# A decoder layer whose split products read their moving tiles backwards, with weight places displaced

## The chip, the cores and the metric

The kernel runs on one core of a Trainium2 chip. The metric is the device time of one execution in microseconds (us). Below, PE is TensorE, PEld its weight load, DVE is VectorE, ACT ScalarE, POOL GpSimd and SP SyncE.

## The reference

The kernel computes one decoder layer for 2 sequences of 512 tokens with 1024 features: a selective-scan (Mamba) block, a cross-attention and a feed-forward part, each added to its input and followed by a layer norm.

```python
def reference(x, ctx, ...):                       # x [2,512,1024], ctx [2,1024,1024]
    # 1: in_proj -> conv over 4 tokens, silu -> x_proj, norms, dt -> scan over 16 states -> gate -> out_proj
    proj = x @ in_proj_w; x1, z = split(proj)
    xc = silu(conv(x1)); dt, B, C = rmsnorms(xc @ x_proj_w.T); dt = softplus(dt @ dt_w + bias)
    h_t = exp(dt_t * A) * h_{t-1} + dt_t * B_t * xc_t;  y_t = h_t . C_t
    x = layernorm(x + ((y + D * xc) * silu(z)) @ out_proj_w.T)
    # 2: 16 query heads of 96 over 4 key/value heads, keys from [ctx, x] (1536 rows)
    x = layernorm(x + softmax(q k^T / sqrt(96)) v @ Wo.T)
    # 3: weights scaled by blocks of 128 x 128, 1024 -> 3584 -> 1024
    x = layernorm(x + (silu(x @ (w1*s1).T) * (x @ (w3*s3).T)) @ (w2*s2).T)
```

All is float32. Products are to come out with more precision than one float32r product gives.

## The kernel before, in words

**Split products.** A float32 operand is split into a part that ACT rounds to float32r (`hi`) and the remainder that DVE or POOL subtracts (`lo`). A product is then three float32r matmuls into one PSUM bank, issued by the helper `three_passes` (line 106): `w_hi` times `x_hi` (L108), `w_hi` times `x_lo` (L109), `w_lo` times `x_hi` (L110). The first operand is the weight tile of 128 columns, loaded before each matmul (PEld); the second is the moving tile, mostly of 512 columns, which streams past it.

**Who uses the helper.** The input projection (`mamba_in`, with the small x_proj product of 96 weight columns among it), the output projection (`steps`), keys, values and queries, attention's probabilities times values, the output projection of attention, and the feed-forward part. Attention's scores (L1961 to L1963) and its row maxima (L1939) are float32r matmuls too, but are issued directly. The scan (L972 to L1019) uses plain float32 matmuls.

**Where the tiles lie.** Each phase places its SBUF tiles one behind another with an `Arena` (line 79), which rounds each tile's size up to 32 bytes. Tiles of the split products are multiples of 512 bytes, so weights and moving tiles lie at the same place modulo 512 bytes in nearly every phase. The exception is the x_proj product, whose weight tiles are 384 bytes long, one behind another (`xpw_hi`, `xpw_lo`).

**Order.** There is no scheduler. Every engine has a function of its own for each phase, with its loops and semaphore waits written out. In the feed-forward part, `NW = 8` slots of `w_hi` and `w_lo` go round: ACT rounds into `w_hi` (L2377, in the second half L2401), DVE subtracts into `w_lo` (L2566, L2614), PE waits for `w_lo_done` and runs 12 matmuls (4 tiles of K, three passes each). The first half makes 7 products per pair of blocks in place of 8, with DVE and POOL making sums of operands and results; the second half reads its operands back from device memory. In `mamba_in` two slots of `w_hi` and `w_lo` go round (L334 on ACT, L407 on DVE), 48 matmuls of PE to each.

Of the kernel before, what the change touches and what calls it, by code (L numbers as in the profile page):

```python
# [22 lines left out]
F32R = mybir.dt.float32r  # L23
# [4 lines left out]
P = 128  # L28
B, L, H = 2, 512, 1024
TOK = B * L  # L30
HT = H // P
# [71 lines left out]
    return ap.bitcast(F32)  # L103


def three_passes(nc, out, w_hi, w_lo, x_hi, x_lo, start, stop):

    nc.tensor.matmul(out, w_hi, x_hi, start=start, stop=False)  # L108
    nc.tensor.matmul(out, w_hi, x_lo, start=False, stop=False)  # L109
    return nc.tensor.matmul(out, w_lo, x_hi, start=False, stop=stop)  # L110
# [92 lines left out]
def mamba_in(nc, res, d, ps_all, scan):  # L203
# [6 lines left out]
    sb = Arena(nc, "in")  # L210
# [8 lines left out]
    x_hi = sb("x_hi", [P, HT, TOK], F32R)  # L219
    x_lo = Arena(nc, "in")("x_lo", [P, HT, TOK], F32R)  # L220
    dtw = Arena(nc, "in_dtw", sb.at)("dtw", [R + 1, IT, P])
    w = [sb(f"w{s}", [P, HT, P]) for s in range(2)]
    w_hi = [sb(f"w_hi{s}", [P, HT, P], F32R) for s in range(2)]
    w_lo = [sb(f"w_lo{s}", [P, HT, P], F32R) for s in range(2)]
    xz = [sb(f"xz{s}", [P, B, L + KC - 1]) for s in range(2)]
    acc = [sb(f"acc{s}", [P, B, L]) for s in range(2)]
    pre = [sb(f"pre{s}", [P, B, L]) for s in range(2)]
# [261 lines left out]
    def tensor(pe):  # L489
        def main(m, s, between=None, at=0):  # L490
            pe.wait_ge(w_lo_done, m + 1)
            pe.wait_ge(left, m)
            for k in range(HT):
                pe.wait_ge(x_lo_done, k + 1)
                if between is not None and k == at:
                    between()
                for b in range(B):
                    c = slice(b * L, (b + 1) * L)
                    last = three_passes(nc, ps[s][:, b], w_hi[s][:, k], w_lo[s][:, k], x_hi[:, k, c], x_lo[:, k, c],
                                        k == 0, k == HT - 1)  # L500
            last.then_inc(main_done, 1)

        def xproj(s, ready, stop=False):
            pe.wait_ge(xc_lo_done, ready)
            pe.wait_ge(xpw_done, ready)
            for b in range(B):
                last = three_passes(nc, ps_xp[:, b], xpw_hi[s][:], xpw_lo[s][:], xc_hi[s][:, b], xc_lo[s][:, b],
                                    False, stop)
            last.then_inc(xproj_done, 1)
# [522 lines left out]
def mamba(nc, res, d, steps):  # L1032
# [3 lines left out]
    scan = mamba_scan(nc, res, d, ps_all, steps)  # L1036
    early = Phase(nc)
    first = mamba_in(nc, early, d, ps_all, scan)

    with nc.Block() as block:  # L1040
# [187 lines left out]
def project_norm_qkv(nc, res, d, ps, heads, steps):  # L1228
# [322 lines left out]
    def tensor(pe):  # L1551
        def step(n):
            s, k = n % 2, n
            pe.wait_ge(steps.lo_done, 2 * n + 2)
            for m in range(HT):
                c = slice(m * P, (m + 1) * P)
                last = three_passes(nc, ps[:, m], steps.w_hi[s][:, c], steps.w_lo[s][:, c], steps.a_hi[s][:], steps.a_lo[s][:], k == 0, k == KT - 1)
                if k == KT - 1:
                    last.then_inc(tile_done, 1)
                    if m == FIRST:  # L1560
                        pe.wait_ge(const_set, 2)
                        pe.wait_ge(v_done, HT + 2)
                        mean(0)
            if k < KT - 1:
                last.then_inc(steps.used, 1)
# [434 lines left out]
def heads_and_feed_forward(nc, res, d, steps, carried, attn, out, ahead):  # L2000
# [7 lines left out]
    with nc.Block() as block:  # L2008
        @block.sync
        def _(sp):  # L2010
            nonlocal forward
            first.sync(sp)
            heads.sync(sp, lambda: (early.release(), carried.release()))

            forward = attention_out_feed_forward(nc, res, d, ps, heads, attn, out, ahead)
            forward.sync(sp)
# [26 lines left out]
def attention_out_feed_forward(nc, res, d, ps, heads, attn, out, ahead):  # L2043
# [11 lines left out]
    NJ = FT // 2  # L2055
    NM = 7
    NW, NX = 8, 4
    sb = Arena(nc, "ff")

    def sem(n):  # L2060
# [4 lines left out]
    x_hi, x_lo, x_at = [None] * NM, [None] * NM, [0] * NM  # L2065
# [36 lines left out]
    w_hi, w_lo = [], []  # L2102
    for s in range(NW):
        if s == NW - 1:
            wo_at = Arena(nc, "ff_wo", sb.at)
        w_hi.append(sb(f"w_hi{s}", [P, HK, P], F32R))
        w_lo.append(sb(f"w_lo{s}", [P, HK, P], F32R))
    p0, u3 = sb("p0", [P, L]), sb("u3", [P, L])
    u2, u4 = ([sb(f"{n}{s}", [P, L]) for s in range(2)] for n in ("u2", "u4"))
    wo[0] = wo_at("wo0", [P, KH, P])  # L2110
# [971 lines left out]
```

## Time and profile before

| | us |
|---|---|
| two runs | 3046.60 and 3050.18, median 3048.39 |
| profiled execution: first to last instruction | 3047.5 |
| PE busy | 2833.3 (93%), 11958 matmuls |
| DVE busy | 2393.1 (79%) |
| POOL busy | 1712.8 (56%) |
| ACT busy | 1574.6 (52%) |

The profile gives the busy time of each engine, the granted clock of TensorE, groups of instructions by line, the waits, and a timeline. The duration of a matmul in it includes its way through the array, and matmuls overlap: how long one occupies the engine is read from the distance between the starts of two.

The phases on PE, from the timeline: input projection up to 220 us, the small dt products up to 318, the scan up to 1114, output projection, keys, values and queries up to 1418, attention up to 2041, its output projection up to 2178, the feed-forward part to the end, its second half from 2748.

### The profile page before, as it was taken

The numbers are of one execution on the slowest core, as the hardware profiler recorded it, in microseconds if no ns is written. First come the engines' busy times: TensorE is split into PE (matmuls) and PEld (weight loads), VectorE is DVE, ScalarE is ACT, GpSimd is POOL, SyncE is SP. The second block draws the span as 40 slices with busy tenths as digits, with TensorE's granted clock in tenths as the row PEclk, the third lists the DMA queues.
The fourth block names the chain that finished last, engine by engine and source line by source line (L and its number), as shares of the span: only waits on it lengthen the run. The fifth ranks groups of instructions, "written<-read, shape, count | busy, mean of one in ns | idle before, by whom it ended". The sixth has DMA issues, their size and how long they took to land. (4 is left out here: it accounts for less than half of the span.)

```text
span 3047.5 us, 35696 instructions
## 1 busy us (share of the span) xinstructions
PE 2833.3 (93%) x11958; PEld 2028.4 (67%) x11958; DVE 2393.1 (79%) x2168; ACT 1574.6 (52%) x2685; POOL 1712.8 (56%) x1035
## 2 busy tenths in 40 slices
PE   8997588888788889999999999999989999999997
PEld 7882244444222348888888888887768888887886
DVE  6558999999999977444777777765988888885677
ACT  4448555555665545213888888873433333334443
POOL 0003999999999953403888888861044444430034
PEclk9995799999999999999999999999989999999999
DMA  4228886666875645232111111215245555567654
GB/s 152 83 83 261 274 200 159 179 171 152 250 219 148 199 150 216 104 119 72 37 37 37 37 37 37 71 54 200 97 156 180 180 179 180 180 218 238 194 176 139
DMA packets 217641, 445.84 MB, mean 146 GB/s; under 512 B 33661, under 2 KB 47741, under 8 KB 215613
## 3 DMA queue, kind: packets, MB, share of 16 engines
q1 hardware_dynamic: 179742, 390.73, 41.1%
q10 hardware_dynamic: 37728, 52.96, 5.3%
q8 instruction: 91, 1.49, 0.2%
q14 instruction: 80, 0.66, 0.1%
HBM read 313.45 MB, written 130.15 MB: 146 GB/s over the span
## 5 line engine op out<-in xcount | busy, mean ns | idle before, releaser
L1927 POOL TENSOR_TENSOR at_p_lo<-at_p,at_p_hi 128x512 fp32r<-128x512 f32 x384 | 514.6, 1348 | 244.3 <-ACT at_p_hi L1820 236.5
L716 POOL TENSOR_TENSOR scan_dbx<-scan_u,scan_b_bc 128x1024 f32<-128x1024 f32 x256 | 596.1, 2359 | 0.0
L885 ACT ACTIVATE mamba_ps<-scan_dt,scan_a_neg 128x512 f32<-128x512 f32 (+1 forms) x512 | 332.0, 680 | 315.1 <-DVE scan_g L903 291.3
L914 DVE TENSOR_TENSOR_SCAN mamba_ps<-mamba_ps,scan_dbx 128x1024 f32<-128x1024 f32 x195 | 440.0, 2283 | 3.1 <-ACT mamba_ps L887 1.7
L1847 DVE TENSOR_REDUCE at_neg_max<-heads_ps 128x1 fp32r<-128x1536 f32 x128 | 224.9, 1757 | 134.4 <-PE heads_ps L1939 132.4
L108 PE MATMUL heads_ps<-ff_x_hi,ff_w_hi 128*128 128x512 f32 x784 | 310.0, 395 | 17.2 <-DVE ff_u L2572 6.4
L2812 POOL TENSOR_TENSOR ff_raw<-ff_raw,ff_scale 128x512 f32<-128x512 f32 x112 | 115.9, 1066 | 361.2 <-DMA ff_raw<-in_w 252.8
L109 PE MATMUL heads_ps<-ff_x_lo,ff_w_hi 128*128 128x512 f32 x784 | 308.1, 393 | 0.0
L110 PE MATMUL heads_ps<-ff_x_hi,ff_w_lo 128*128 128x512 f32 x784 | 308.1, 393 | 0.0
L1816 ACT ACTIVATE at_p<-heads_ps 128x512 f32<-128x512 f32 x384 | 228.2, 594 | 110.0 <-PE heads_ps L1963 95.8
L1820 ACT ACTIVATE at_p_hi<-at_p 128x512 fp32r<-128x512 f32 x384 | 242.8, 632 | 12.2
L989 PE MATMUL mamba_ps<-scan_x,scan_wz 128*128 128x512 f32 x448 | 212.5, 618 | 23.8 <-ACT scan_zb L805 16.7
L903 DVE TENSOR_TENSOR scan_g<-mamba_ps,scan_c_bc 128x1024 f32<-128x1024 f32 x195 | 234.2, 1201 | 0.0
L1019 PE MATMUL mamba_ps<-scan_g,scan_sel 128*32 128x512 f32 x1024 | 138.9, 613 | 81.3 <-DVE scan_g L903 67.5
L989 PEld LDWEIGHTS mamba_ps<-scan_x,scan_wz 128*128 128x128 f32 x448 | 82.7, 194 | 155.7 <-issue 129.0
L108 PEld LDWEIGHTS heads_ps<-ff_x_hi,ff_w_hi 128*128 128x128 f32 x784 | 149.1, 190 | 51.5 <-DVE ff_u L2572 7.4
L109 PEld LDWEIGHTS heads_ps<-ff_x_lo,ff_w_hi 128*128 128x128 f32 x784 | 149.2, 190 | 31.5 <-issue 0.5
L110 PEld LDWEIGHTS heads_ps<-ff_x_hi,ff_w_lo 128*128 128x128 f32 x784 | 149.0, 190 | 31.3
L2377 ACT ACTIVATE ff_w_hi<-heads_ps 128x512 fp32r<-128x512 f32 x112 | 66.9, 598 | 197.2 <-DVE heads_ps L2561 183.7
L108 PE MATMUL heads_ps<-ff_hs_hi,ff_w_hi 128*128 128x512 f32 x392 | 154.7, 395 | 7.3 <-DVE ff_act_h L2601 3.7
L929 POOL TENSOR_TENSOR scan_g<-scan_g,scan_c_bc 128x1024 f32<-128x1024 f32 x61 | 144.2, 2365 | 24.5 <-DVE scan_g L914 24.4
L110 PE MATMUL heads_ps<-ff_hs_hi,ff_w_lo 128*128 128x512 f32 x392 | 153.8, 392 | 0.0
(306 smaller groups left out, 6906.8 us busy)
## 6 DMA issues: line engine op xcount, KB each, us to landing
scan_dt<-dt SPq DMA_DIRECT2D x120, 256.0 KB, 4.8
scan_u<-u SPq DMA_DIRECT2D x120, 256.0 KB, 7.6
ff_raw<-in_w SPq DMA_DIRECT2D x56, 512.0 KB, 4.6
ff_down_ar<-ac SPq DMA_DIRECT2D x98, 256.0 KB, 2.8
ff_down_hr<-hc SPq DMA_DIRECT2D x98, 256.0 KB, 2.7
ff_act_w<-in_w SPq DMA_DIRECT2D x14, 1024.0 KB, 7.6
hc<-ff_act_t SPq DMA_DIRECT2D x56, 256.0 KB, 6.2
ac<-ff_act_v SPq DMA_DIRECT2D x56, 256.0 KB, 5.9
```

What stands on the lines that cost most here:

```text
L108: nc.tensor.matmul(out, w_hi, x_hi, start=start, stop=False)
L109: nc.tensor.matmul(out, w_hi, x_lo, start=False, stop=False)
L110: return nc.tensor.matmul(out, w_lo, x_hi, start=False, stop=stop)
L716: nc.gpsimd.tensor_tensor(dbx[n % SL][:].rearrange("p (h l) -> p h l", h=2), u[it % 2][:, c:c + 2], b_bc[b][:, k // 2].unsqueeze(1).to_bro ...
L885: nc.scalar.activation(at[:, h * L + h:(h + 1) * L], dt[it % 2][:, c, h:L], ACT.Exp, scale=a_neg[:, it % IT, e:e + 1]).then_inc(a_ready, 1)
L903: nc.vector.tensor_tensor(g[n % SG][:].rearrange("p (h l) -> p h l", h=2), ps_a[n % SA].rearrange("p (h l) -> p h l", h=2), c_bc[n // (NP ...
L914: nc.vector.tensor_tensor_scan(out[:], ps_a[n % SA], dbx[n % SL][:], 0.0, ALU.mult, ALU.add).then_inc(scanned, 1)
L989: last = nc.tensor.matmul(ps_x, wz[q % ZC][:, k], x[:, k, b * L:(b + 1) * L], start=k == 0, stop=k == HT - 1)
L1816: nc.scalar.activation(p[t % NSL][:], ps_s[t % 2], ACT.Exp, scale=SCALE).then_inc(exp_done, 1)
L1820: nc.scalar.activation(p_hi[t % NSL][:], p[t % NSL][:], ACT.Copy).then_inc(p_hi_done, 1)
L1847: nc.vector.tensor_reduce(neg_max[:, i, HD:HD + 1], ps_mx.rearrange("p n l -> p (n l)"), AX_X, ALU.max, negate=True).then_inc(max_done, 1)
L1927: nc.gpsimd.tensor_tensor(p_lo[n % NSL][:], p[n % NSL][:], f32(p_hi[n % NSL][:]), ALU.subtract).then_inc(p_lo_done, 1)
```

## The change

It has two parts. `three_passes` views its output and both moving tiles from the last column to the first (`[:, ::-1]`), so that the moving tile is read, and the PSUM bank written, backwards; each result lands where it did. And weight places are displaced: in `mamba_in` the four slots get 64 bytes more room and begin 16, 48, 4 and 8 bytes into it (`w_hi0`, `w_lo0`, `w_hi1`, `w_lo1`); in the feed-forward part each of the sixteen places is followed by 32 bytes, so that they lie 0, 32, 64, ... 480 bytes past a multiple of 512. `align()` brings what follows back to a multiple of 512. No instruction is added, removed or moved on any engine, and no wait changes.

```diff
+def back(ap):
+    return ap[:, ::-1]
+
 def three_passes(nc, out, w_hi, w_lo, x_hi, x_lo, start, stop):
 
+    out, x_hi, x_lo = back(out), back(x_hi), back(x_lo)
     nc.tensor.matmul(out, w_hi, x_hi, start=start, stop=False)
     nc.tensor.matmul(out, w_hi, x_lo, start=False, stop=False)
     return nc.tensor.matmul(out, w_lo, x_hi, start=False, stop=stop)
...
-    w_hi = [sb(f"w_hi{s}", [P, HT, P], F32R) for s in range(2)]
-    w_lo = [sb(f"w_lo{s}", [P, HT, P], F32R) for s in range(2)]
+    w_hi, w_lo = [], []
+    for s in range(2):
+        for part, name, by in ((w_hi, "w_hi", (16, 4)[s]), (w_lo, "w_lo", (48, 8)[s])):
+            wide = sb(f"{name}{s}", [P, HT * P + 16], F32R)
+            part.append(wide[:, by // 4:by // 4 + HT * P].rearrange("p (k m) -> p k m", m=P))
...
+    STEP = 32
...
     for s in range(NW):
         if s == NW - 1:
-            wo_at = Arena(nc, "ff_wo", sb.at)
+            wo_at = Arena(nc, "ff_wo", sb.at).align()
         w_hi.append(sb(f"w_hi{s}", [P, HK, P], F32R))
+        sb.at += STEP
         w_lo.append(sb(f"w_lo{s}", [P, HK, P], F32R))
+        sb.at += STEP
+    sb.align()
```

## Rows read from the trace of the kernel before

**Rows 1.** Page: busy time, clock by fortieths, the chain that ended last by line.
```profile
PE 2833.3 (93%) x11958; PEld 2028.4 (67%) x11958; DVE 2393.1 (79%) x2168; ACT 1574.6 (52%) x2685; POOL 1712.8 (56%) x1035
...
PEclk9995799999999999999999999999989999999999
...
PE heads_ps L108 9%; PE heads_ps L110 9%; PE heads_ps L109 9%; DVE ff_w_lo L2614 1%; DVE ff_hs_lo L2617 1%; PE heads_ps L2998 0%; DVE ff_x_lo L2539 0%; DVE ff_y L2543 0%; DVE ff_norm_rstd L1187 0%; DMA ff_wo_wo<-in_w_o 0%; DVE ff_wo_wo_lo L2522 0%; DVE ff_y L1193 0%; DVE ff_w_lo L2566 0%; POOL ff_raw L2812 0%; ACT ff_x_hi L2356 0%
```

**Rows 2.** Busy time by stretch, columns as in its head.
```profile
core 0: us, PE busy (x) PEld busy (x) DVE busy (x) ACT busy (x) POOL busy (x), PEclk, DMA share, GB/s
10.00:220.00 210.00, 210.00 (x922) 170.42 (x921) 125.68 (x121) 95.86 (x90) 10.12 (x16) 1.00 0.27 94
...
1418.00:2041.00 623.00, 621.61 (x2802) 511.75 (x2800) 458.36 (x303) 518.23 (x874) 514.64 (x384) 1.00 0.14 41
2041.00:2228.00 187.00, 172.03 (x711) 136.06 (x712) 145.94 (x197) 73.54 (x106) 9.91 (x8) 0.97 0.42 145
2228.00:2985.00 757.00, 747.21 (x3268) 616.34 (x3268) 594.42 (x792) 265.45 (x450) 285.02 (x200) 0.99 0.57 192
```

**Rows 3.** The busiest stretch of DVE, same columns.
```profile
2400.00:2640.00 240.00, 240.00 (x1061) 198.79 (x1060) 210.31 (x281) 74.93 (x125) 112.78 (x82) 1.00 0.53 183
```

**Rows 4.** PE groups by line: count, busy us, mean ns, idle before.
```profile
L108 PE MATMUL heads_ps<-ff_x_hi,ff_w_hi 128*128 128x512 f32 x784 | 310.0, 395 | 17.2 <-DVE ff_u L2572 6.4 <-DVE ff_x_lo L2539 5.8 <-ACT ff_act_h L2396 5.0
...
L108 PE MATMUL heads_ps<-ff_hs_hi,ff_w_hi 128*128 128x512 f32 x392 | 154.7, 395 | 7.3 <-DVE ff_act_h L2601 3.7 <-DVE ff_hs_lo L2617 3.7
```

**Rows 5.** Line L108 alone in the stretches before 318 and behind 1114.
```profile
10.00:220.00 210.00, 119.89 (x307) 1.00 0.27 94
220.00:318.00 98.00, 5.86 (x14) 0.60 0.75 250
...
1114.00:1206.00 92.00, 51.57 (x128) 0.96 0.76 274
1206.00:1418.00 212.00, 116.89 (x304) 0.98 0.28 95
1418.00:2041.00 623.00, 149.55 (x384) 1.00 0.14 41
2041.00:2228.00 187.00, 94.39 (x231) 0.97 0.42 145
2228.00:2985.00 757.00, 426.31 (x1089) 0.99 0.57 192
2985.00:3047.50 62.50, 19.94 (x48) 0.90 0.37 124
```

**Rows 6.** Timeline of PE, feed-forward: start us, duration, first and last of 178 matmuls.
```profile
2599.79 0.39 PE L109 MATMUL heads_ps<-ff_x_lo,ff_w_hi 128*128 128x512 f32 x1
...
2639.91 0.39 PE L109 MATMUL heads_ps<-ff_x_lo,ff_w_hi 128*128 128x512 f32 x1
```

**Rows 7.** Timeline, one matmul and the weight load beside it.
```profile
2700.20 0.39 PE L108 MATMUL heads_ps<-ff_x_hi,ff_w_hi 128*128 128x512 f32 x1
2700.20 0.19 PEld L109 LDWEIGHTS heads_ps<-ff_x_lo,ff_w_hi 128*128 128x128 f32 x1
```

**Rows 8.** Timeline of PE, output projection, where the clock rises.
```profile
1118.16 0.63 PE L110 MATMUL heads_ps<-step_a_hi,step_w_lo 128*128 128x512 f32 x1
...
1119.87 0.63 PE L108 MATMUL heads_ps<-step_a_hi,step_w_hi 128*128 128x512 f32 x1
...
1120.61 0.40 PE L110 MATMUL heads_ps<-step_a_hi,step_w_lo 128*128 128x512 f32 x1
...
1121.32 0.39 PE L110 MATMUL heads_ps<-step_a_hi,step_w_lo 128*128 128x512 f32 x1
1121.54 0.39 PE L108 MATMUL heads_ps<-step_a_hi,step_w_hi 128*128 128x512 f32 x1
...
1122.70 0.39 PE L110 MATMUL heads_ps<-step_a_hi,step_w_lo 128*128 128x512 f32 x1
```

**Rows 9.** Timeline of PE, x_proj: first of six matmuls, and what follows them.
```profile
33.22 0.39 PE L108 MATMUL mamba_ps<-in_xc_hi,in_xpw_hi 128*96 128x512 f32 x1
...
34.60 0.39 PE L108 MATMUL mamba_ps<-in_x_hi,in_w_hi 128*128 128x512 f32 x1
```

**Rows 10.** Writers in the input projection, 10 to 220 us: count, busy us, mean ns, idle before.
```profile
L334 ACT ACTIVATE in_w_hi<-in_w 128x1024 fp32r<-128x1024 f32 x17 | 17.9, 1052 | 0.1
...
L358 ACT ACTIVATE in_xz<-mamba_ps 128x1024 f32<-128x1024 f32 x16 | 16.5, 1028 | 21.1 <-PE mamba_ps L110 21.1
```

## The prediction

> **What bounds the kernel.** I began with the page: PE is busy 93% of the span, DVE 79%, and the chain that ended last names the three lines of the helper, L108 to L110, as its largest parts; the clock is near full nearly everywhere [rows 1]. Then the stretches. Outside the scan, PE is busy 210.0 of 210 us in the input projection, 621.6 of 623 in attention and 747.2 of 757 in the feed-forward part [rows 2]. Where DVE is busiest it has 210.3 of 240 us, PE all of them [rows 3]. So outside the scan time is the number of matmuls times the distance between two starts. The idle time before L108 shows how little PE waits: 17.2 and 7.3 us over the feed-forward part's two halves [rows 4].
>
> The helper's matmuls: L108 runs 307 + 14 + 128 + 304 + 384 + 231 + 1089 + 48 = 2505 times [rows 5], with L109 and L110 7,515 in all. None is in the scan.
>
> The distance is what the change can touch. Between the first and the last of 178 matmuls lie 177 distances: 2639.91 − 2599.79 = 40.12 us, 226.7 ns each [rows 6]. At full clock (2.4 GHz) 512 columns, one a cycle, need 213.3 ns. At the lower clock (1.2 GHz) four distances take 1119.87 − 1118.16 = 1.71 us, 427 ns each, and 512 columns need 426.7: nothing is added there [rows 8]. So at full clock each matmul pays 13.4 ns above its columns, at half clock none. What goes on beside it is the next weight load, which begins with the matmul and lasts 190 ns whatever happens [rows 7]: moving reads and weight reads fall in the same time.
>
> Two rows say that this surcharge depends on how the two streams lie to each other. Behind the rise of the clock the same operands have distances of 0.22 and 0.24 us in turn, (1122.70 − 1120.61) / 9 = 232 ns on average, before they settle at 226.7 [rows 8]. And the x_proj product, whose weight tiles don't lie at the moving tile's place modulo 512 bytes, needs (34.60 − 33.22) / 6 = 230 ns, with fewer weight columns (96) to load [rows 9]. I read this as weight reads taking turns from moving reads at the same part of SBUF, and the aligned placement before as one that settles into a fairly good rhythm.
>
> **The change, part by part.** *Reading backwards.* Counts, order and waits stay. The compiled program reads weights from the last column down. Before, the two streams run against each other; now both run down, the moving one about twice as fast. They meet fewer times during a load, but may stay together longer when they do. No row of before has this. Its value is bounded by rows: below by the columns alone, 213.3 ns (13.4 saved; a gain is not excluded, since half clock shows it), above by the worst distances seen between unsettled streams, 0.24 us, of which the averages are 230 and 232 [rows 8, 9]. I take 220, the middle between 226.7 and 213.3: half of the surcharge goes. It also matches the best single distance of before, 0.22 us between 1121.32 and 1121.54 [rows 8], which shows that a better rhythm exists.
>
> Full clock holds for about 7,400 of the 7,515: the granted clock of 0.96 to 0.99 in the stretches behind 1114 [rows 5] means some 50 us at half clock, about 120 matmuls. Saved: 7,400 × 6.7 ns = 49.6 us.
>
> The direct float32r matmuls of attention keep 226.7, but for those beside which a helper's weights load.
>
> *Displacing the feed-forward places.* It changes where 1,176 × 3 helper matmuls' weights (784 + 392) [rows 4] lie to their moving tiles, in sixteen ways. By itself it could undo the rhythm, as in x_proj: that price is in the bounds above. Writers stay at multiples of 32 bytes, as x_proj's do; I add nothing.
>
> *Displacing the input projection's places by 4 to 48 bytes.* ACT and DVE now write and read there off a 32-byte multiple. The nearest row is L358, which writes 12 bytes off and takes 1028 ns against 1052 for L334 [rows 10]: no price. Even 5% on both would lie under PE, with ACT busy 96 and DVE 126 of 210 us [rows 2].
>
> *What is late next.* With 3% less PE time, DVE's 210 of 240 us becomes 210 of 233 [rows 3]; DVE doesn't bind on average, but single waits such as those before L108 [rows 4] grow. I give back 2 us.
>
> Sum: 49.6 − 2 = 48 us less. The profiled span is 3047.5, 0.9 under the median of the runs, 3048.4; from the median, 3000.
>
> **What the Trainium skill says.** By its page "TensorE: Matmul & The Clock Gate" (Step-by-step), TensorE has two independent read ports, and loading weights doesn't take read bandwidth from the running matmul. By that rule direction and place change nothing; this is the third case below. The trace disagrees with its number: it gives 215.7 ns between matmuls of 512 columns, the rows 226.7. The page "Advanced Engine Details and Errata" (PSUM Cachelines) says that an access pattern of PSUM that isn't contiguous slows matmuls significantly; neighbours remain neighbours here, but no row shows a descending write, and the last case below is what it would do.
>
> **The rivals.**
> 1. *The surcharge goes almost wholly*: 213.3 to 217.5 ns. Both streams go the same way, and once one is past the other they don't meet again. For it: half clock shows no surcharge. Against: x_proj shows that merely moving places doesn't do it. At 215.5: 7,400 × 11.2 = 83 us, less 5 given back to DVE: 2970.
> 2. *Slower: the rhythm is lost.* With the moving stream in step with the weight stream, they contend for a whole stretch of a load, and with displaced places the matmul never settles, as behind the clock's rise and in x_proj. At 232 ns: 7,400 × 5.3 = 39 us more, 3087; it decides from 226.7 up, the worst (236) gives 3117. For it: two of three placements in the rows are worse than the aligned one. Against: nothing says that direction breaks the rhythm.
> 3. *No change*: the surcharge is a fixed cost of a float32r weight load (32 cycles for 128 columns), direction and place don't matter. 225 to 229 ns: 3036 to 3065. Against it: 0.22 to 0.24 us for the same operands [rows 8].
> 4. *A descending stream runs at half rate*: 427 ns, as at half clock [rows 8], 7,400 × 0.2 us more: some 4530. For it only that no row excludes it.
>
> **How the numbers follow.** Chances: the forecast (217.5 to 225 ns, 2982 to 3036) 46%, nearly all gone 21%, no change 17%, slower by a lost rhythm 13%, half rate 3%. The predicted time is the likeliest case's. The range 2962 to 3072 leaves out the lower end of rival 1 (4%), most of rival 2 (10%) and rival 4. A measurement here tells 2%, 61 us, from no change. Faster by over 61 us needs 218.4 ns or less: rival 1 and the edge of the forecast, 29%. Slower by over 61 us needs 235 or rival 4: 6%. Within: 65%.
>
> **What would show it.** Right: in the feed-forward part 178 matmuls span about 38.9 us in place of 40.12; all float32r weight loads keep 190 ns; L1961 and L1939 keep 226.7 and the scan its time; PE stays busy all through attention and the feed-forward part. Distances that differ by slot of the ring would show that the displacement matters, equal ones that direction does. Wrong: distances of 230 or more; or distances as forecast with DVE waits before L108 that eat the gain.

## The result

| | us, median (lowest to highest) | ratio to the kernel before, 95% interval |
|---|---|---|
| kernel before | 3048.39 (3046.6 to 3050.18) | |
| changed kernel | 3101.42 (3100.01 to 3102.83) | 1.0171 (1.0142 to 1.0201) |

The changed kernel is 53 us slower, where 48 us less were forecast. Its profiled execution spans 3098.7 us against 3047.5, 51.2 us more.

The page of the changed kernel, in the form of [rows 1]:

```profile
PE 2892.5 (93%) x11958; PEld 2034.8 (66%) x11958; DVE 2384.7 (77%) x2168; ACT 1579.3 (51%) x2685; POOL 1710.6 (55%) x1035
...
PEclk9995799999989999999999999999989999999999
...
PE heads_ps L114 10%; PE heads_ps L115 9%; PE heads_ps L116 9%; DVE ff_w_lo L2627 1%; DVE ff_hs_lo L2630 1%; DVE ff_x_lo L2552 0%; DVE ff_y L2556 0%; PE heads_ps L3011 0%; POOL ff_raw L2825 0%; DVE ff_y L1202 0%; PE heads_ps L1156 0%; DVE ff_norm_rstd L1196 0%; DVE ff_sum_y L2814 0%; DVE ff_w_lo L2579 0%; POOL ff_end_total_sq L2899 0%
...
L114 PE MATMUL heads_ps<-ff_x_hi,ff_w_hi 128*128 128x512 f32 x784 | 316.8, 404 | 15.8 <-DVE ff_u L2585 6.5
...
L114 PE MATMUL heads_ps<-ff_hs_hi,ff_w_hi 128*128 128x512 f32 x392 | 158.4, 404 | 6.3 <-DVE ff_act_h L2614 3.5
```

PE is busy 59 us longer with the same 11,958 matmuls, of which the span shows 51, since PE idles 8 us less; DVE, ACT and POOL have what they had to within 9 us, and the clock row is the same but for one slice. The chain still consists of the helper's three lines, now L114 to L116. The waits before the first of them have become shorter, from 17.2 and 7.3 us to 15.8 and 6.3 [rows 4]. So no wait and no engine beside PE took the time: each matmul takes longer.

The stretch of [rows 3] again:

```profile
2400.00:2640.00 240.00, 240.00 (x1029) 193.11 (x1028) 200.00 (x269) 73.91 (x123) 110.05 (x80) 1.00 0.52 178
```

The timeline of PE in the feed-forward part, as [rows 6] (start us, duration us), first and last of 173 matmuls:

```profile
2649.69 0.40 PE L116 MATMUL heads_ps<-ff_x_hi,ff_w_lo 128*128 128x512 f32 x1
...
2689.86 0.40 PE L114 MATMUL heads_ps<-ff_x_hi,ff_w_hi 128*128 128x512 f32 x1
```

The weight load there, from the timeline of PE's loads, as [rows 7]:

```profile
2649.93 0.19 PEld L115 LDWEIGHTS heads_ps<-ff_x_lo,ff_w_hi 128*128 128x128 f32 x1
```

PE is busy all of 240 us in both kernels, at a granted clock of 1.00, but gets through 1029 matmuls where it did 1061. Between the first and the last of the 173 matmuls lie 172 distances: 40.17 us, 233.5 ns each, against 226.7 [rows 6]. The weight load keeps its 0.19 us [rows 7]. At full clock (2.4 GHz) 226.7 ns are 544 cycles, 32 above the 512 columns; 233.3 ns are 560, or 48 above. So what a matmul takes above its columns, the surcharge, grew by a half; the forecast had it halved.

Where the clock rises, in the output projection, the changed kernel looks like this (PE, start us, duration us), to be read beside [rows 8]:

```profile
1124.36 0.63 PE L115 MATMUL heads_ps<-step_a_lo,step_w_hi 128*128 128x512 f32 x1
...
1126.49 0.45 PE L114 MATMUL heads_ps<-step_a_hi,step_w_hi 128*128 128x512 f32 x1
1126.78 0.40 PE L115 MATMUL heads_ps<-step_a_lo,step_w_hi 128*128 128x512 f32 x1
...
1131.91 0.40 PE L116 MATMUL heads_ps<-step_a_hi,step_w_lo 128*128 128x512 f32 x1
```

At half clock five distances take 1126.49 − 1124.36 = 2.13 us, 426 ns each: reading backwards costs nothing there, just as the surcharge was nil before. At full clock the 22 distances from 1126.78 on take 5.13 us, 233.2 ns each, from the first one. There is no unsettled stretch that settles later; this is the steady state.

By stage, from the timelines (us; distances are medians of the helper's matmuls in the stage, in whole ns, as the trace has the starts). The input projection is taken up to the first of the small dt products, at 231.5 us in the kernel before, not to the 220 us named ahead:

| stage | before | after | more | distance before | after |
|---|---|---|---|---|---|
| input projection | 231.5 | 238.4 | 6.9 | 227 | 233 |
| dt and scan | 883.1 | 884.1 | 1.0 | | |
| output projection | 91.9 | 93.5 | 1.6 | 227 | 233 |
| keys, values, queries | 211.7 | 216.7 | 5.0 | 227 | 233 |
| attention | 623.5 | 637.3 | 13.8 | 227 | 231 to 240 by line |
| its output projection | 135.6 | 138.1 | 2.5 | 227 | 233 |
| feed-forward, first half | 570.2 | 584.9 | 14.7 | 227 | 231 to 236 by slot and line |
| feed-forward, second half | 300.0 | 305.7 | 5.7 | 227 | 231 to 236 by slot and line |

The scan has plain float32 matmuls and doesn't use the helper: nothing happened there. Every other stage pays.

Attention pays more than its share, since there both directions occur. The timeline of PE before, the first direct matmuls of a group:

```profile
1600.04 0.39 PE L1961 MATMUL heads_ps<-at_q_hi,at_k_hi 128*128 128x512 f32 x1
1600.27 0.39 PE L1962 MATMUL heads_ps<-at_q_lo,at_k_hi 128*128 128x512 f32 x1
1600.50 0.39 PE L1963 MATMUL heads_ps<-at_q_hi,at_k_lo 128*128 128x512 f32 x1
```

The same piece of the changed kernel, with the helper's three behind it:

```profile
1602.08 0.40 PE L1970 MATMUL heads_ps<-at_q_hi,at_k_hi 128*128 128x512 f32 x1
1602.32 0.39 PE L1971 MATMUL heads_ps<-at_q_lo,at_k_hi 128*128 128x512 f32 x1
1602.55 0.39 PE L1972 MATMUL heads_ps<-at_q_hi,at_k_lo 128*128 128x512 f32 x1
1602.78 0.40 PE L114 MATMUL heads_ps<-at_p_hi,at_v_hi 128*128 128x512 f32 x1
1603.01 0.40 PE L115 MATMUL heads_ps<-at_p_lo,at_v_hi 128*128 128x512 f32 x1
1603.25 0.40 PE L116 MATMUL heads_ps<-at_p_hi,at_v_lo 128*128 128x512 f32 x1
```

L1970 to L1972 are the old L1961 to L1963, and are themselves not reversed. Still the distance from L1970 to L1971 went from 0.23 to 0.24 us (median 227 to 238 ns over 384 pairs). The distances behind the helper's three lines sum to 8.3 us more, near the 1,152 × 6.7 ns = 7.7 us that a flat rise would give; those behind the direct matmuls, which the change doesn't touch, sum to another 5.6 us, 2.0 of it in the row maxima.

### The profile page after: what moved, and what is told of

It is laid out like the page before. It is cut to its first block and busy times, and to the rows that moved or that the text cites. A ratio compares the mean times of both kernels' runs of the same rounds, so it can differ in the third digit from the quotient of the medians.

```text
span 3098.7 us, 35696 instructions
## 1 busy us (share of the span) xinstructions
PE 2892.5 (93%) x11958; PEld 2034.8 (66%) x11958; DVE 2384.7 (77%) x2168; ACT 1579.3 (51%) x2685; POOL 1710.6 (55%) x1035
## 5 line engine op out<-in xcount | busy, mean ns | idle before, releaser
L114 PE MATMUL heads_ps<-ff_x_hi,ff_w_hi 128*128 128x512 f32 x784 | 316.8, 404 | 15.8 <-DVE ff_u L2585 6.5
L115 PE MATMUL heads_ps<-ff_x_lo,ff_w_hi 128*128 128x512 f32 x784 | 314.9, 402 | 0.0
L116 PE MATMUL heads_ps<-ff_x_hi,ff_w_lo 128*128 128x512 f32 x784 | 314.3, 401 | 0.0
L114 PEld LDWEIGHTS heads_ps<-ff_x_hi,ff_w_hi 128*128 128x128 f32 x784 | 149.6, 191 | 55.1 <-DVE ff_u L2585 7.4
L115 PEld LDWEIGHTS heads_ps<-ff_x_lo,ff_w_hi 128*128 128x128 f32 x784 | 149.7, 191 | 36.4 <-issue 0.5
L116 PEld LDWEIGHTS heads_ps<-ff_x_hi,ff_w_lo 128*128 128x128 f32 x784 | 149.4, 191 | 36.5
L114 PE MATMUL heads_ps<-ff_hs_hi,ff_w_hi 128*128 128x512 f32 x392 | 158.4, 404 | 6.3 <-DVE ff_act_h L2614 3.5
L115 PE MATMUL heads_ps<-ff_hs_lo,ff_w_hi 128*128 128x512 f32 x392 | 157.6, 402 | 0.0
```

## The experiments

Two theories stood after the result. **Direction:** reading the moving tile from its last column down is what costs, whatever the places. **Places:** the displaced weights cost, and direction does little or even helps. Behind them stood a third question, whether it is the read or the backward write into PSUM, and whether the weight load has a part in it at all.

**Reading backwards alone**, all places as before:

```diff
+def back(ap):
+    return ap[:, ::-1]
...
 def three_passes(nc, out, w_hi, w_lo, x_hi, x_lo, start, stop):
 
+    out, x_hi, x_lo = back(out), back(x_hi), back(x_lo)
```

> Kernel before with the moving tiles and PSUM output of the helper reversed, all places as before. Theory A (direction: both streams going down settle into a dearer rhythm): 233.3 ns between helper matmuls in every phase, 3095 to 3101 us. Theory B (the displaced places cost it): the distance stays 226.7 in the input projection and the feed-forward part, and the time is 3048 to 3065.

3098.93 us (3096.67 to 3102.04), ratio 1.0166 (1.015 to 1.0183). That is the whole loss of the change: the intervals of the two ratios overlap. Outside attention, where they are as in the change, the helper's distances are 233.0 to 233.9 ns in every stage. The stretch of [rows 3] holds 1030 matmuls:

```profile
2400.00:2640.00 240.00, 240.00 (x1030) 193.40 (x1029) 200.46 (x272) 73.47 (x123) 109.21 (x78) 1.00 0.51 176
```

**The displaced places alone**, nothing reversed (the diff of the change without the line above):

> Kernel before with the weight places of the change, nothing reversed. Theory A: output projection, queries and attention keep 226.7 ns; input projection and feed-forward part between 226.7 and 232 ns, since place alone may disturb the rhythm: 3048 to 3072 us. Theory B: 233 to 236 ns in the displaced phases, 3080 to 3090.

3073.79 us (3071.39 to 3074.6), ratio 1.0081 (1.0064 to 1.0097). Only the stages with displaced weights lose: the input projection 6.1 us (237.6), the feed-forward halves 12.6 and 6.3 (582.8 and 306.3). The other stages keep their times within 0.8 us, but for the scan, which varies by more from run to run (796 to 800 us over all these kernels). The stretch of [rows 3], with 1033 matmuls:

```profile
2400.00:2640.00 240.00, 240.00 (x1033) 193.75 (x1032) 200.34 (x271) 73.56 (x122) 111.68 (x80) 1.00 0.50 174
```

The timeline of PE there, first and last of 174 matmuls, 173 distances of 232.6 ns:

```profile
2599.63 0.39 PE L115 MATMUL heads_ps<-ff_x_hi,ff_w_lo 128*128 128x512 f32 x1
...
2639.87 0.40 PE L114 MATMUL heads_ps<-ff_x_lo,ff_w_hi 128*128 128x512 f32 x1
```

So places cost 26 us by themselves (3073.79 against 3047.94 of the kernel before beside it), yet they add nothing that the times can tell once the read is backwards (3101.42 against 3098.93, ranges 3100.01 to 3102.83 and 3096.67 to 3102.04). The traces still show a little of them: in the feed-forward part the mean distances by slot and line lie between 231.8 and 235.9 ns in the changed kernel, between 233.2 and 233.5 with the read backwards alone. Over all slots that is 233.6 against 233.3, some 1 us for the 3,528 matmuls. The two parts are not a sum, which asks for a look at one matmul alone.

**Series of matmuls.** This and three more kernels compute no layer. Each ran once. They run series of 40 equal float32r matmuls (128 × 128 weights, 512 moving columns unless said otherwise), each with its weight load, on one input tile. A series' distance is the mean of its last 20 distances between starts. The first one crosses direction with the weights' displacement from a multiple of 512 bytes:

```python
def forward(nc, out, w, x):
    return nc.tensor.matmul(out, w, x, start=True, stop=True)
def backward(nc, out, w, x):
    return nc.tensor.matmul(out[:, ::-1], w, x[:, ::-1], start=True, stop=True)
def read_back_alone(nc, out, w, x):
    return nc.tensor.matmul(out, w, x[:, ::-1], start=True, stop=True)
def write_back_alone(nc, out, w, x):
    return nc.tensor.matmul(out[:, ::-1], w, x, start=True, stop=True)
```

> Not the layer: a series of 40 float32r matmuls each with one weight tile and one moving tile in SBUF, forward and backward (moving and output), with the weight tile displaced by 0 to 480 bytes, then moving alone or output alone reversed, then fewer weight columns or moving columns. Theory A (weight reads take turns from moving reads): forward at 0 bytes 226.7 ns, backward at 0 bytes 233.3, the value changes with displacement in both, moving alone reversed like backward, output alone reversed like forward. Rival C (a descending PSUM write is what costs): output alone reversed 233.3, moving alone 226.7. Rival D (a fixed cost per float32r weight load): the same at every displacement. With 64 weight columns the surcharge halves under A (about 6.7 ns), stays under a fixed cost.

The timeline of PE merges each series to one row; two letters name the weights' place (aa is 0, ba 32, ca 64 bytes and so on to ia, 256). The difference of two starts, divided by 40, is the distance. Forward (L14), backward (L18), read alone (L22), output alone (L26). The first of these views ends at 110 us, and its last row with it:

```profile
18.82 9.24 PE L14 MATMUL mps<-mx,w_aa 128*128 128x512 f32 x40
27.90 9.49 PE L14 MATMUL mps<-mx,w_ba 128*128 128x512 f32 x40
37.22 9.50 PE L14 MATMUL mps<-mx,w_ca 128*128 128x512 f32 x40
...
74.54 9.33 PE L14 MATMUL mps<-mx,w_ga 128*128 128x512 f32 x40
83.71 9.49 PE L14 MATMUL mps<-mx,w_ha 128*128 128x512 f32 x40
93.04 9.24 PE L14 MATMUL mps<-mx,w_ia 128*128 128x512 f32 x40
102.11 8.09 PE L14 MATMUL mps<-mx,w_ja 128*128 128x512 f32 x34
...
260.21 9.50 PE L18 MATMUL mps<-mx,w_aa 128*128 128x512 f32 x40
269.55 9.50 PE L18 MATMUL mps<-mx,w_ba 128*128 128x512 f32 x40
...
502.89 9.49 PE L22 MATMUL mps<-mx,w_aa 128*128 128x512 f32 x40
512.23 9.50 PE L22 MATMUL mps<-mx,w_ba 128*128 128x512 f32 x40
...
540.23 9.26 PE L26 MATMUL mps<-mx,w_aa 128*128 128x512 f32 x40
549.32 9.49 PE L26 MATMUL mps<-mx,w_ba 128*128 128x512 f32 x40
```

Forward at 0 bytes: (27.90 − 18.82) / 40 = 227 ns. At 32 bytes: 233. At 256 bytes again (102.11 − 93.04) / 40 = 227. All places, settled distance in ns:

| bytes past a multiple of 256 | 0 | 32 | 64 | 96 | 128 | 160 | 192 | 224 |
|---|---|---|---|---|---|---|---|---|
| forward | 226.7 | 233.3 | 233.3 | 234.2 | 232.4 | 233.4 | 229.1 | 233.3 |
| backward | 233.3 | 233.3 | 233.3 | 233.3 | 233.3 | 233.3 | 233.3 | 233.3 |

The forward row repeats from 256 to 480 bytes to 0.1 ns, and 4 to 28 bytes cost 230.0 to 235.0. This one table gives both layer runs in sum. Backward, no place matters with one weight tile of 128 columns: hence the change costs what its first part costs. Forward, the mean over the eight places is 232.0 ns; the feed-forward part's 3,528 helper matmuls at 5.3 ns more are 18.7 us, and its halves lost 12.6 + 6.3 = 18.9. Matmul by matmul the table doesn't hold there: tiles of different places take turns, and the mean distances by slot and line run from 229.1 to 238.1 ns, 232.6 over all, which would be 20.8 us: the nearness of 18.7 to 18.9 is luck in part. The read alone reversed (L22) costs 233.3 ns; the output alone reversed (L26) costs 227 at 0 bytes, as forward does. So it is the read of the moving tile, and the PSUM write is free.

The last series of this kernel have fewer columns, with the weights at 0 bytes (ns):

| | 96 weight columns | 64 | 32 | 384 moving columns | 256 |
|---|---|---|---|---|---|
| forward | 230.0 | 229.5 | 231.7 | 173.3 | 120.0 |
| backward | 236.7 | 233.3 | 233.3 | 177.6 | 118.3 |

The surcharge doesn't halve with 64 weight columns, as weight reads that take turns all through a load would have it. And backward is not dearer everywhere: with 256 moving columns it is the cheaper order by 1.7 ns.

The Trainium skill's page "Advanced Engine Details and Errata" (PSUM Cachelines) has every non-contiguous pattern slow matmuls down; for an order of descending neighbours the L26 row shows no such cost.

**Which order of the moving columns costs.** The second series kernel displaces moving tiles, varies sizes and types, and reads in blocks:

```python
    def blocks_down(m):
        run(ws[0][:], x[:, 0:L].rearrange("p (a b) -> p a b", b=m)[:, ::-1, :])
...
    def blocks_up_inside_down(m):
        run(ws[0][:], x[:, 0:L].rearrange("p (a b) -> p a b", b=m)[:, :, ::-1])
```

> Not the layer: series of 40 matmuls, each of one weight tile and one moving tile, output always forward. Theory A2 (reads of the moving tile and of the next weights meet at the same part of SBUF, by place modulo 256 bytes, and the descending order of the moving read settles at 233.3 ns): both tiles displaced together keeps 226.7; the moving tile displaced alone gives what the weights displaced the other way gave (230 to 234); bfloat16 and plain float32, which take half the bytes per cycle, show no surcharge at any place or direction (216 and 427 to 429). Blocks of moving columns taken in descending order but read forward inside: small blocks (16 bytes) near 233, blocks of 256 bytes and more near 227. Theory E (the surcharge is the start of a matmul, not the reading): blocks make no difference but for the first column; 8 weight columns cost as much as 128 (about 13 to 18 ns over the columns); the surcharge is the same for 128 and 512 moving columns. If alternating weight tiles of two displacements gives under 226.7, a version faster than the kernel before exists.

| columns in a block | 2 | 4 | 8 | 16 | 32 | 64 | 128 | 256 |
|---|---|---|---|---|---|---|---|---|
| blocks descending, forward inside | 233.3 | 233.3 | 233.3 | 233.3 | 232.3 | 226.7 | 226.7 | 226.7 |
| blocks ascending, backward inside | 226.7 | 226.7 | 233.3 | 266.6 | 233.3 | 233.3 | 233.3 | 233.3 |

64 columns are 256 bytes, the same period as with the places. Whether whole blocks of 256 bytes come up or down doesn't matter; the order within them does, and the worst order of this table, ascending blocks of 64 bytes read backwards, costs 640 cycles instead of 544. Displacing the moving tile counts like displacing the weights the other way (moving tile at 64 bytes 229.1 ns, as the weights at 192), and displacing both together costs nothing (starts of PE; x_b,w_b has both at 32 bytes, x_c,w_c both at 64, x_b,w_a the moving tile alone at 32; the view ends at 218 us):

```profile
170.38 9.28 PE L45 MATMUL mps<-x_b,w_b 128*128 128x512 f32 x40
179.50 9.25 PE L45 MATMUL mps<-x_c,w_c 128*128 128x512 f32 x40
188.59 9.27 PE L45 MATMUL mps<-x_e,w_e 128*128 128x512 f32 x40
...
206.81 9.48 PE L45 MATMUL mps<-x_b,w_a 128*128 128x512 f32 x40
216.13 2.22 PE L45 MATMUL mps<-x_c,w_a 128*128 128x512 f32 x9
```

(188.59 − 179.50) / 40 = 227 ns, against (216.13 − 206.81) / 40 = 233. So what counts is how the moving read lies to the weight read. A plain float32 matmul is two records of 429 ns each in the trace (160 for the 80 matmuls of two series), so 858 ns, in either direction. Fewer weight columns at 0 bytes, forward: 8 to 120 of them take 228.8 to 233.6 ns, in this kernel and the one before, never the 226.7 of 128.

**Blocks of 64 columns in descending order, in the layer:**

```diff
+def turned(ap):
+    return ap.rearrange("p (a b) -> p a b", b=64)[:, ::-1, :]
...
+    out, x_hi, x_lo = turned(out), turned(x_hi), turned(x_lo)
```

> Kernel before, with the helper's moving tiles and output taken in blocks of 64 columns (256 bytes), the last block first, each block forward inside. If what counts is the order of reads within 256 bytes (series of the shapes: 226.7 ns with such blocks), 3048 us as before. If it is the descent over the whole tile, 233.3 ns and about 3099.

3048.16 us (3046.32 to 3054.42) against 3049.29 of the kernel before beside it, ratio 1.0001 (0.9992 to 1.0011).

```profile
2400.00:2640.00 240.00, 240.00 (x1060) 198.72 (x1059) 210.16 (x280) 74.93 (x125) 112.91 (x82) 1.00 0.54 183
```

The moving tiles are read from high addresses to low over their whole length, in steps of 256 bytes, and the loss of 50 us is gone.

**Ascending blocks of 16 columns, backward inside**, the same diff with `b=16` and `[:, :, ::-1]`:

> Kernel before, with the helper's moving tiles and output taken in ascending blocks of 16 columns (64 bytes), each read backwards inside. The series of shapes gave 266.7 ns for it: 7,400 matmuls by 40 ns are 296 us, 3330 to 3345 us, if the whole kernel follows the series. If the kernel's distance is set by something the series doesn't have, 3048 to 3100.

3327.36 us (3325.55 to 3328.24), ratio 1.0911 (1.0892 to 1.0929). Timeline of PE, feed-forward part:

```profile
2799.74 0.43 PE L114 MATMUL heads_ps<-ff_x_hi,ff_w_hi 128*128 128x512 f32 x1
...
2839.74 0.43 PE L114 MATMUL heads_ps<-ff_x_hi,ff_w_hi 128*128 128x512 f32 x1
```

151 matmuls, 150 distances, 266.7 ns: the series' value to the tenth, in the layer, and slightly less in all than a flat sum gives: 7,400 × 40 ns = 296 us, where some 278 came. The page shows where the rest went:

```profile
PE 3129.2 (94%) x11958; PEld 2059.3 (62%) x11958; DVE 2375.7 (71%) x2168; ACT 1579.3 (47%) x2685; POOL 1699.7 (51%) x1035
```

PE is busy 295.9 us more than before and idles 16.5 us less, among it the waits before L114 in the feed-forward part (17.2 and 7.3 us before, 14.2 and 3.5 here).

**The weight slots of the input projection and the feed-forward part displaced by 256 bytes**, forward (against the changed kernel; the reversing line is out too):

```diff
-        for part, name, by in ((w_hi, "w_hi", (16, 4)[s]), (w_lo, "w_lo", (48, 8)[s])):
-            wide = sb(f"{name}{s}", [P, HT * P + 16], F32R)
+        for part, name, by in ((w_hi, "w_hi", (256, 256)[s]), (w_lo, "w_lo", (256, 256)[s])):
+            wide = sb(f"{name}{s}", [P, HT * P + 64], F32R)
...
-    STEP = 32
+    STEP = 0
...
+    sb.at += 256
```

> Kernel before, reading forward, with every helper weight place of the input projection and the feed-forward part displaced by 256 bytes. If the place counts modulo 256 bytes, as in the grid, 3048 us (same). If any displacement from the moving tile's place modulo 512 costs, about 3074, as with the change's places alone.

3047.83 us (3044.48 to 3049.7), ratio 0.9996 (0.9986 to 1.0006): no change, with 1060 matmuls in the stretch of [rows 3] again. Beside the places of 4 to 480 bytes, which cost 1.0081, this confirms the period in the layer.

**Few weight columns, few moving columns, mixed directions:**

```python
    def few_at(off, m, back):
        run(ws[off][:, 0:m], x[:, 0:L][:, ::-1] if back else x[:, 0:L])

    def both_few(w, m):
        run(ws[0][:, 0:w], x[:, 0:m])

    def mixed(p):
        run(ws[0][:], [x[:, 0:L][:, ::-1] if c == "b" else x[:, 0:L] for c in p])
```

> Not the layer: series of 40 matmuls. Theory F (the surcharge arises once per matmul, where a new moving read and a new weight load begin, not per weight read): with 8 weight columns the place modulo 256 bytes and the direction still matter (226 to 236 ns), and with 64 to 448 moving columns and 8 weight columns the distance is the columns at 2.4 GHz plus 13 to 18 ns. Theory A3 (weight reads take turns all through the load): with 8 weight columns all places and directions come to within 3 ns of 215. Mixed directions: a matmul that differs in direction from its neighbour costs up to 240 ns, as seen in attention. No series below 226.7 ns at 512 columns.

PE's timeline, 8 weight columns, w_b to w_h at 32 to 224 bytes; from 96.20 on backward:

```profile
31.49 9.41 PE L45 MATMUL mps<-xa,w_b 128*8 128x512 f32 x40
40.74 9.41 PE L45 MATMUL mps<-xa,w_c 128*8 128x512 f32 x40
...
96.20 9.50 PE L45 MATMUL mps<-xa,w_a 128*8 128x512 f32 x40
105.54 9.49 PE L45 MATMUL mps<-xa,w_b 128*8 128x512 f32 x40
...
325.87 17.44 PE L45 MATMUL mps<-xb,wb 128*128 128x512 bf16 x80
343.15 17.43 PE L45 MATMUL mps<-xb,wbc 128*128 128x512 bf16 x80
```

A load of 8 columns, 88 ns long in the trace where one of 128 takes 188 to 190, leaves 231 ns forward displaced and 233 backward, and 226.7 forward at 0 bytes. So the surcharge doesn't shrink with the weight columns. But the same 8 columns at 0 bytes had settled at 230.8 ns in the series of shapes: what a series settles at is not fixed by its operands alone, and what else it depends on is open. The surcharge grows with the moving columns: 8 weight columns with 64, 128, 256 and 512 moving columns take 30, 60, 115.7 and 226.7 ns, that is 3.3, 6.7, 9.0 and 13.4 above one cycle a column (the 60 is from the kernel of other orders below, since here that series ran at half clock, at 106.7 ns, which is its columns alone). So both ideas put ahead miss in part: 8 weight columns don't come to 215 ns, and the surcharge of few moving columns is not the 13 to 18 ns of 512. bf16 has (343.15 − 325.87) / 80 = 216 ns, in both directions and at both places tried. Forward and backward in turn take 236.7 ns on average with single distances up to 240, which is near attention's L1970 (238) and L115 (240) in the changed kernel. Two forward and one backward in turn take 233.4.

The Trainium skill's "TensorE: Matmul & The Clock Gate" (Step-by-step) gives 215.7 ns from matmul to matmul and two independent read ports. For bf16 the rows agree with both, 216 ns wherever the weights lie. For float32r they don't: 226.7 ns at best, and 233.3 by the weights' place alone, where reads that don't touch each other would give one value. What couples them is not shown.

**Other orders, as a search for less than 226.7:**

```python
    def spread(h, k):
        run(ws[0][:], x[:, 0:L].rearrange("p (h c k) -> p c h k", h=h, k=k))

    def two_places(delta, k):
        v = x[:, 0:2 * delta].rearrange("p (h c) -> p h c", h=2)[:, :, 0:L // 2]
        run(ws[0][:], v.rearrange("p h (c k) -> p c h k", k=k))
```

> Not the layer: series of 40 matmuls that read the same 512 moving columns in another order: runs of k columns taken in turn from h places of the tile, and from two places whose distance is 0, 32, 64, 128 or 192 bytes off a multiple of 256. Theory G (the moving read itself is a little too slow for one 4-byte column per cycle at 2.4 GHz, and how slow depends on the order of reads within 256 bytes): distances differ by order, between 216 and 270 ns, and an order under 226.7 ns may exist; were there one at 220 or less, the layer could gain 50 us. Rival H (226.7 is the floor of every order): none under 226.7.

Runs of 4 to 64 columns taken in turn from 2 to 16 places took between 226.7 and 278 ns. None came under 226.7, nor did any series of the other three kernels with 512 float32r columns, though single distances of 224 stand in some. So no version that beats the kernel before came out of this; those of the same speed are the blocks of 64 and the places by 256 bytes.

## Why the prediction was wrong

*What bounds the kernel* held. PE is the end of every stage outside the scan, time is the number of matmuls times their distance, and a change of the distance went into the span almost undiminished: the forecast's 7,400 matmuls times the measured 6.7 ns more are 49.6 us; the span grew by 51.2. That the two lie so near is luck in part: PE's busy time grew by 59.2 us, 5.6 of it in direct matmuls that the forecast left as they were, and 8.0 came back from shorter idle time.

*The surcharge* held as a row: 13.4 ns above the columns at full clock, none at half clock, and none at half clock backwards either. Two readings beside it did not hold. The 230 ns of x_proj was laid to the place of its weights, but a series with 96 weight columns at 0 bytes takes 230.0 ns too, so the row doesn't tell place from column count. And the weight load doesn't last 190 ns whatever happens: at half clock it takes 0.33 us (timeline of PE's loads before):

```profile
1118.16 0.33 PEld L108 LDWEIGHTS heads_ps<-step_a_hi,step_w_hi 128*128 128x128 f32 x1
```

*The step that failed* is "They meet fewer times during a load ... I take 220", under *Reading backwards*. It took the surcharge for a contention of two streams that is counted by their meetings, with the weight read as one side. Measured: backward 233.3 ns in place of 220, which turns −49.6 us into +49.6. The idea of meetings, counted over the whole tile as it was there, is contradicted by two findings. A load of 8 weight columns in place of 128 leaves the surcharge. And the direction of the whole tile doesn't matter when blocks of 256 bytes stay forward inside (3048 us in the layer). The best single distance of before, 0.22 us, was no sign of a better rhythm either: it belongs to a pair of 0.22 and 0.24, and no steady series ran under 226.7. The midpoint of two bounds had no row for it; 213.3 was a bound that no order reached. What the runs don't exclude is a contention counted another way, by place modulo 256 bytes, since the moving read's place counts relative to the weights'. What had been named as a sign of being wrong, distances of 230 or more, is what came.

*"The direct float32r matmuls of attention keep 226.7, but for those beside which a helper's weights load"* failed with its reason. L1970 to L1971 rose to 238 ns, and what loads beside it are the weights of L1971, another direct matmul. L1972, beside which the helper's weights do load, kept 227 ns. The others rose with the read backwards alone too (238 ns) and kept 227 with the places alone, and the series in turn reaches 240: it is the neighbourhood of backward reads. It was a term of 5.6 us, put at nothing.

*The displaced feed-forward places* were given no price of their own but the bounds of x_proj and the rise of the clock, 230 and 232. As a size those rows were good: 232.0 in the series, 18.9 us in the layer. But they were laid to a rhythm that can be lost. It is a steady cost by place, modulo 256 bytes and relative to the moving tile, and for backward reads next to nothing is left of it (233.6 against 233.3 ns in the feed-forward part). *The input projection's places* needed no term in the change (its stage takes 238.4 us with them, 238.1 with the read backwards alone); alone they cost 6.1 us, on PE and not on the writers that were looked at there.

*What is late next* was right in kind: DVE doesn't bind on average. With PE slower its waits shrank, by 1.4 and 1.0 us before L114.

*The rivals.* The second, slower, named 232 ns and 3087 us and got 13%: in number it is nearest (233.3; 3101), and it sits at the right place, displaced or reversed streams. Its mechanism, a rhythm that never settles, is not what the rows show, since in the series the backward distance is the steadiest of all (233 or 234 ns each once it has settled). No gain and no 215.5 came of the first; the third (fixed cost) fell to the forward table; the fourth, half rate, to 233.

## What to carry to other kernels

Where a kernel is bound by one short operation that runs thousands of times, a forecast about its inside is worth little: a series of 40 such operations repeats to a tenth of a ns within a run, and it gave the layer runs of either part to within a few us here. It needs the layer's own shapes and neighbours: one pair of operands settled at 226.7 and at 230.8 ns in different runs, and directions taken in turn cost more than either alone. For float32r products of 512 moving and 128 weight columns, keep moving and weight tiles at the same place modulo 256 bytes and read the moving one forward within 256 bytes (226.7 ns against up to 235, and 266.7 in the worst order carried into the layer). A value between two bounds that no row supports should not carry the likeliest case.

## What the hardware showed unexpectedly

- Several settled distances for 512 float32r columns are whole cycles at 2.4 GHz: 544, 560, 576 and 640 (226.7, 233.3, 240.0 and 266.7 ns). They are means: forward with the weights at 12 bytes, single distances of 224 and 236 take turns. In bf16 the surcharge is under 3 ns, in plain float32 likewise for each of a matmul's two records (429 ns, two cycles a column), at half clock nil for float32r in either direction.
- It depends on the order of the moving columns within 256 bytes and on the place relative to the weights modulo 256 bytes; backward, with 128 weight columns, the place doesn't matter. With 256 moving columns backward is cheaper than forward (118.3 against 120.0 ns). Reversal within 4 columns (16 bytes) costs nothing. The Trainium skill's "Advanced Engine Details and Errata" (SBUF Cachelines) has lines of 16 bytes, which that last number fits (226.7 with groups of 4 reversed inside, 233.3 with groups of 8), but not the period of 256 bytes.
- What in SBUF or in TensorE makes it is open. The runs exclude the PSUM write and show no shrinking with a shorter weight load. They don't exclude the weight load as such, since no float32r matmul ran without one.
- A forward matmul beside a backward one can be dearer than either among its own kind: up to 240 ns, 236.7 on average when they take turns. It need not be: L1972, with a backward one behind it, kept 227.
